# Second part of a perceiver kernel: one block for both parts, matmul work in slots of one gated unit, two chunks routed a slot

## The chip, the cores and the metric

The kernel runs on one core of a Trainium2 chip. A core has five engines that run their own instruction streams and meet at semaphores: PE (TensorE, matmuls), ACT (ScalarE), DVE (VectorE), POOL (GpSimd) and SP (SyncE), which here only issues DMAs. DMAs move data between HBM and the on-chip memory (SBUF); matmuls write to eight banks of PSUM. The metric is device time of one execution in microseconds (us), lower is better.

## The reference

One layer of a perceiver on 64 sequences of 32 tokens with D = 256, all in float32. It has three residual steps; the third, called part 2 here, is what the change is about:

```
x = x + xattn(layernorm(x), ctx)        # cross attention to 257 context rows and the own 32
x = x + mix_and_moe(layernorm(x))       # recurrent time mix, then 8 experts, 2 a token
x = x + ffn(layernorm(x))

geglu(x, w1, w2, w3) = gelu(x @ w1) * (x @ w2) @ w3
def ffn(xf):                            # xf: 2048 tokens x 256
    shared = geglu(xf, w1s, w2s, w3s)   # 256 -> 1024 -> 256
    idx = argmax(xf @ Wg)               # one of 8 experts
    final = sum over e of where(idx == e, geglu(xf, W1[e], W2[e], W3[e]), 0)
    return shared + final
```

## The kernel before

Tokens are worked on in 16 chunks of 128. A first block does the attention, the mix and the 39 tiles of the second step's experts, whose results go to a table rows_y in HBM. It ends with a clearing of its semaphores and a barrier of all engines (L1466). Part 2 follows in three more blocks.

A **unit** is the gated work on 128 tokens: `hidden` on PE (two halves, each of 8 matmuls for x @ w1 and then 8 for x @ w2; the profile counts two records a matmul, so 64 in all), `gelus` on ACT, `products` on DVE (L1708), `down` on PE (L1715, 8 matmuls, 16 records). There are 16 shared units, one a chunk, and 23 routed units, one for each tile of 128 places in the lists of the experts, since lists are rounded up to whole tiles. That makes 39 units.

*Block C* goes over the chunks one at a time, in 18 steps. For chunk a, POOL copies two columns of row numbers (L1754) and gathers the two expert results of the chunk from rows_y (L1757, ya and yb). DVE adds them, weighted, to x (L1810, L1813), takes mean and variance (L1816 to L1821), POOL raises to the power -0.5 (L1762), and DVE writes the normed chunk z (L1828). PE transposes z (L1777), ACT copies it to zT_c (L1800), PE multiplies by the router's matrix (L1785), and DVE copies the 8 scores (L1834). SP stores z to rows_z. On PE the order inside a step is: hidden of the chunk before, transposes of this chunk, down of the chunk before that, router of this chunk. The loop does 12 shared units; four chunks' transposed inputs are kept for later.

*Block `routing`* (L1487 on) takes all scores at once: the largest, the ranks inside each expert, the numbers of tiles, and the table of each tile's tokens, which PE builds with matmuls of one-hot matrices (L1546). One shared unit runs on PE between its steps. No routed unit can start before its end, as neither its expert nor its tokens are known.

*Block F* runs one shared unit, the 23 routed ones, then two shared ones. SP loads the three matrices of a tile's expert, 1 MB each (L1893). POOL gathers a tile's rows from rows_z (zr, ahead by up to four), PE transposes them, and hidden and down follow. Results go to rows_f. POOL gathers from it for all 16 chunks, when the last tile is stored (L1931), DVE adds (L2018), and SP stores the output (L1913).

The loops are written with `sweep`, which peels some steps and runs the rest in a hardware loop; the order on each engine is as written in `body`, and no planner moves it.

## Time and profile before

| | us |
|---|---|
| median of 3 runs (lowest to highest) | 973.64 (972.09 to 974.47) |
| the profiled execution, its own time | 966.43 |
| its span | 964.7 |
| first hidden of part 2 starts | 498.84 |
| last down of part 2 ends | 954.2 |
| PE busy in the span | 858.3 |

The span goes from the first to the last instruction of the profiled execution; 1.7 us of its own time lie around it. The median of the runs shown is 7.2 us above it. The profile has a row of the matmul clock that the chip granted, in tenths or as a fraction of full speed, and a row of how busy the 16 DMA engines were. Rows of the timeline give the start, the busy time, the engine, the source line and the operation; in brackets stands how long the engine had been idle and what ended that. A matmul's modelled end overlaps the start of the next, so lengths are best read from start to start.

### The profile page before, as it was taken

What the parts mean: (1) busy time and instruction counts of PE and PEld (TensorE: products, weight loads), DVE (VectorE), ACT (ScalarE), POOL (GpSimd) and SP (SyncE); (2) the same over time, 40 slices, a digit from 0 to 9 for tenths busy, and PEclk for the clock granted to TensorE, in tenths of its full rate; (3) what the DMA queues carried; (4) which work ended last, traced back from release to release, by engine and by line L of the source; (5) the groups of instructions that cost most, each with busy time, mean ns of one, the idle gap of its engine ahead of it and who ended that gap; (6) DMA issues with size and microseconds to landing.
All of it is one profiled execution on the core that took longest, in us unless ns stands there. A gap on an engine that the chain in (4) does not pass through costs nothing. (4 is left out here: it accounts for less than half of the span.)

```text
span 964.7 us, 19179 instructions
## 1 busy us (share of the span) xinstructions
PE 858.3 (89%) x6306; PEld 768.6 (80%) x6306; DVE 445.0 (46%) x1253; ACT 316.3 (33%) x712; POOL 349.3 (36%) x605
## 2 busy tenths in 40 slices
PE   5899989886667999999949999968999999999994
PEld 4567766665566889999849999957999999999993
DVE  1279989888774555555523333353111111111113
ACT  1466767664542445555411111100111111111110
POOL 1445677766775355544142222211100010000006
PEclk9899999998688989999979999989999999999998
DMA  9875557534612322263121111102998988999716
GB/s 355 277 268 189 194 112 233 155 103 188 169 43 53 79 67 83 83 214 84 50 66 33 34 38 40 38 28 73 336 330 305 329 301 324 303 319 306 270 61 175
DMA packets 92096, 161.79 MB, mean 168 GB/s; under 512 B 13832, under 2 KB 71112, under 8 KB 88680
## 3 DMA queue, kind: packets, MB, share of 16 engines
q1 hardware_dynamic: 71008, 103.39, 32.2%
q10 hardware_dynamic: 12832, 37.82, 10.5%
q0 software_dynamic: 8176, 19.57, 7.9%
q8 instruction: 43, 0.70, 0.3%
q14 instruction: 37, 0.30, 0.1%
HBM read 146.10 MB, written 14.66 MB: 167 GB/s over the span
## 5 line engine op out<-in xcount | busy, mean ns | idle before, releaser
L1691 PEld LDWEIGHTS bank<-zT_f,we 128*128 128x128 f32 x1472 | 167.9, 192 | 1.8 <-ACT zT_f L1979 0.7
L1691 PE MATMUL bank<-zT_f,we 128*128 128x128 f32 x1472 | 168.2, 275 | 0.5 <-ACT zT_f L1979 0.5
L1708 DVE TENSOR_TENSOR hT_f<-bank,act_g 128x512 f32<-128x512 f32 x78 | 53.8, 691 | 227.6 <-PE bank L1691 208.0
L1700 ACT ACTIVATE act_g<-bank 128x512 f32<-128x512 f32 x78 | 46.6, 597 | 320.4 <-PE bank L1691 320.4
L1691 PE MATMUL bank<-zT_c,a_x 128*128 128x128 f32 x1024 | 121.4, 281 | 0.3 <-PEq L1521 0.3
L1691 PEld LDWEIGHTS bank<-zT_c,a_x 128*128 128x128 f32 x1024 | 119.2, 197 | 0.8 <-issue 0.7
L361 POOL DMA_INDIRECT arena_a<-rows_e,pick x78 | 76.0, 975 | 29.8 <-issue 29.8
L410 PE MATMUL bank<-arena_b,arena_a 128*128 128x128 f32 x624 | 81.8, 288 | 1.6 <-DVE hT L546 1.6
L1715 PE MATMUL bank<-we,hT_f 128*128 128x256 f32 x368 | 83.2, 379 | 0.0
L410 PEld LDWEIGHTS bank<-arena_b,arena_a 128*128 128x128 f32 x624 | 78.2, 204 | 2.4 <-DVE arena_b L538 2.4
L1715 PEld LDWEIGHTS bank<-we,hT_f 128*128 128x128 f32 x368 | 68.1, 190 | 8.3
L437 PE MATMUL bank<-arena_a,hT 128*128 x312 | 73.8, 379 | 0.7 <-DVE arena_a L552 0.7
L1920 POOL COPY pick_f<-table 128x1 uint32 (+1 forms) x23 | 4.2, 184 | 186.3 <-PE bank L1941 159.1
L437 PEld LDWEIGHTS bank<-arena_a,hT 128*128 128x128 f32 x312 | 59.2, 190 | 9.2 <-issue 1.1
L1715 PE MATMUL bank<-t_w,hT_f 128*128 128x256 f32 x256 | 59.9, 388 | 3.7 <-DVE hT_f L1708 3.7
L827 PE MATMUL bank<-arena_b,t_w 128*128 128x128 f32 x384 | 55.3, 298 | 6.8 <-DVE arena_b L1230 3.5
L827 PEld LDWEIGHTS bank<-arena_b,t_w 128*128 128x128 f32 x384 | 49.7, 207 | 13.0 <-issue 13.0
L1715 PEld LDWEIGHTS bank<-t_w,hT_f 128*128 128x128 f32 x256 | 48.6, 195 | 10.5 <-DVE hT_f L1708 4.3
L538 DVE SCALAR_TENSOR_TENSOR arena_b<-arena_b,mu_e 128x128 f32<-128x128 f32 x156 | 44.4, 347 | 6.5 <-issue 6.3
L464 ACT ACTIVATE arena_a<-arena_a 128x1024 f32 x39 | 41.2, 1057 | 10.7 <-issue 10.6
L1762 POOL TENSOR_TENSOR rs<-var,eps_pow 128x1 f32<-128x1 f32 x16 | 9.1, 571 | 93.2 <-DVE var L1821 93.2
L1931 POOL DMA_INDIRECT x<-rows_f,slot x16 | 15.5, 970 | 73.5 <-DMA rows_f<-yr 68.9
(273 smaller groups left out, 1361.8 us busy)
## 6 DMA issues: line engine op xcount, KB each, us to landing
we<-in_W_dram SPq DMA_DIRECT2D x69, 1024.0 KB, 7.4
arena_a<-in_ctx_n_dram ACTq DMA_DIRECT2D x16, 1152.0 KB, 7.2
arena_a<-in_ctx_t_dram SPq DMA_DIRECT2D x16, 1028.0 KB, 9.0
rows_y<-arena_a ACTq DMA_DIRECT2D x39, 128.0 KB, 1.7
arena_a<-in_w_moe_dram ACTq DMA_DIRECT2D x3, 1156.0 KB, 5.3
arena_a<-in_w_moe_dram ACTq DMA_DIRECT2D x3, 1152.0 KB, 7.5
rows_f<-yr ACTq DMA_DIRECT2D x23, 128.0 KB, 6.3
rows_e<-arena_b SPq DMA_DIRECT2D x64, 32.0 KB, 4.0
```

Source lines behind the costliest of these rows:

```text
L361: nc.gpsimd.indirect_dma_start(out=pair[:, n % NM, i * D:(i + 1) * D], out_offset=None, in_=rows_e.ap()[0:rows + 1, :], in_offset=bass.Ind ...
L410: last = nc.tensor.matmul(bMH[:, f * P:(f + 1) * P], wk_e[:, n % 2, k * FK + f * P:k * FK + (f + 1) * P], xk[:, n % 2, k * P:(k + 1) * P], ...
L437: last = nc.tensor.matmul(bMY[:, 0:D], hT[:, n % 2, f * P:(f + 1) * P], ewv_sb[:, e, f * D:(f + 1) * D], start=f == 0, stop=f == FKC - 1)
L464: nc.scalar.activation(wk_e[:, n % 2], ewk_sb[:, e], ACT.Copy).then_inc(m_awk, 1)
L538: last = nc.vector.scalar_tensor_tensor(o[:, n % 2, h], diffT[:, n % 2, h], mu_e[:, n % NM, i, k:k + 1], prevT[:, n % 2, h], ALU.mult, ALU ...
L827: last = nc.tensor.matmul(bank[:, m * P:(m + 1) * P], t_w[:, i, k, m * P:(m + 1) * P], xm[:, n % 2, i, k], start=k == 0, stop=k == KD - 1)
L1691: last = nc.tensor.matmul(bank[half][:, f * P:(f + 1) * P], w12[:, i, k, col0:col0 + P], zT[:, k], start=k == 0, stop=k == KD - 1)
L1700: nc.scalar.activation(act_g[:, half], bU[half][:], ACT.Gelu).then_inc(self.ac_g, 1)
L1708: nc.vector.tensor_tensor(hT[:, parity, half * HH:(half + 1) * HH].rearrange("p f t -> p (f t)"), bG[half][:], act_g[:, half], ALU.mult).t ...
L1715: last = nc.tensor.matmul(bY[parity][:, 0:D], hT[:, parity, f], w3[:, f], start=f == 0, stop=f == HC - 1)
L1762: nc.gpsimd.tensor_tensor(rs4[:, b.slot], var4[:, b.slot], eps_pow[:], ALU.pow).then_inc(po_r, 1)
L1931: nc.gpsimd.indirect_dma_start(out=yg[:, c], out_offset=None, in_=rows_f[:, :], in_offset=bass.IndirectOffsetOnAxis(ap=slot2[:, 0, c:c + 1 ...
```

## The change

The three blocks and the barrier go. Part 2 is written as functions that follow the first part's on each engine, inside the same block, with semaphores of its own or counted on. All loops are written out. PE works in 39 **slots** of one unit each: 11 shared, 23 routed, 5 shared. In the first nine slots it also does the routing's work for one **group** of chunks: groups are (0), (1), (2, 3), ... (14, 15), so a slot takes one chunk in slots 0 and 1 and two in slots 2 to 8.

Ranks are now found slot by slot. DVE finds each chunk's expert, and PE multiplies the one-hot mask, and a running sum over earlier chunks, by two constant matrices (`ranks`). That gives a token's rank in its expert's list. POOL scatters the token's number into a table in HBM (tab_f), in which each expert has a region of its own, and SP later reads a tile's 128 numbers from it (pick_rows), which needs where each tile begins (`tile_map`, on DVE in slot 8). In the first part the picks of a tile are counted on other semaphores, and one DMA more zeroes tab_f.

POOL's gathers for group i + 2 run in slot i. The even chunk's two wait for PE's first mark of the slot (g_pe_u, raised when the first quarter of hidden is done), the odd chunk's for the second, three quarters through hidden; the scatters wait for the end of the down of that slot (g_pe_y). The final gathers are marked the same way over the last five slots, and the last chunk's output is added last by `take`.

The diff, cut to its core:

```
-            for i in range(NM):
-                sp.wait_ge(m_put[i], NT1 // NM * 16)
...
-        nc.clear_and_free_semaphores(one_sems)
-        nc.all_engine_barrier()
...
-        SHARED_C = G - KEPT
-            CSTEPS, CPEEL, CTAIL = G + 2, 5, 5
-        routing("r2_", 1, NT2, logits2, False, table2, expert2, slot2, None, None, ge)
...
+        GROUPS = [(0, 1), (1, 2)] + [(c, c + 2) for c in range(2, G, 2)]
+        NGR = len(GROUPS)
+        NT2 = (TOK - E) // P + E
+        SLOTS = ([("s", c) for c in range(NGR + 2)] + [("r", n) for n in range(NT2)]
+                 + [("s", c) for c in range(NGR + 2, G)])
...
+            def pick_rows(n):
+                at = sp.value_load(place2[0:1, n:n + 1], min_val=0, max_val=T_ROWS // P - 1)
+                sp.dma_start(pick2[:, n], tab_f[bass.ds(at * P, P), :]).then_inc(got_pick[n][0], 16)
+            sp.wait_ge(c_dv_map, 1)
+            sp.wait_ge(c_po_tab, 16 * G)
+            for n in range(AHEAD):
+                pick_rows(n)
+            for n in range(NT2):
+                load_w12(n)
+                if n + AHEAD < NT2:
+                    pick_rows(n + AHEAD)
+                if n > 0:
...
+        def part2_pool(pool):
+            for i in range(NM):
+                pool.wait_ge(m_put[i], NT1 // NM * 16)
+            pool.wait_ge(m_row, 1)
+            def gather_sums(g, i=None, half=None):
+                for c in range(*GROUPS[g]):
+                    if half not in (None, c % 2):
+                        continue
+                    if half is not None:
+                        pool.wait_ge(g_pe_u, i * 2 + 1 + half)
+                    for k, t in enumerate((ya, yb)):
+                        nc.gpsimd.indirect_dma_start(out=t[:, c], out_offset=None, in_=rows_y[:, :],
+                                                     in_offset=bass.IndirectOffsetOnAxis(ap=slot1[:, k, c:c + 1], axis=0)
+                                                     ).then_inc(got_sum[g][0], 16)
...
+            def list_rows(g):
...
+                pool.wait_ge(*((g_pe_y, g) if g else (g_pe_g, 2)))
...
+            gather_sums(0)
+            gather_sums(1)
+            rstd(0)
+            for i in range(NGR):
+                if i + 2 < NGR:
+                    gather_sums(i + 2, i, 0)
+                if i + 1 < NGR:
+                    rstd(i + 1)
+                if i + 2 < NGR:
+                    gather_sums(i + 2, i, 1)
+                list_rows(i)
+            pool.wait_ge(c_put, G * 16)
+            for n in range(NT2):
+                pool.wait_ge(*got_pick[n])
...
+            for (lo, hi), (landed, _) in zip(Y_PARTS, got_y):
+                for c in range(lo, hi):
+                    if c % 2 == 0:
+                        half = UNIT_R[NT2 - 1] * 2 + 4 + c // 2
+                        pool.wait_ge(*((g_pe_g, half + 1) if half < 2 * NSLOT - 2 else (g_pe_u, half)))
...
+            def ranks(g):
+                lo, hi = GROUPS[g]
+                pe.wait_ge(c_dv_mask, g + 1)
+                for c in range(lo, hi):
+                    o = bL[:, (2 + c - lo) * E:(3 + c - lo) * E]
+                    nc.tensor.matmul(o, before_m[:], mask2[:, c], start=True, stop=False)
+                    if c > lo:
...
+            transposed(0)
+            pe.wait_ge(ld_s, 16 * 4)
+            router(0)
+            for i in range(NSLOT):
+                hidden(i, 0)
+                if i < NGR:
+                    ranks(i)
+                hidden(i, 1)
+                if i + 1 < NGR:
+                    transposed(i + 1)
+                if in_slot(i + 1, "r") is not None:
+                    transpose_z(in_slot(i + 1, "r"))
+                if i > 0:
+                    down(i - 1)
+                if i + 1 < NGR:
+                    router(i + 1)
+            down(NSLOT - 1)
...
+            combine(0)
+            normed(0)
+            for i in range(NSLOT):
+                if i >= 2:
+                    take(i - 2)
+                if i + 1 < NGR:
+                    combine(i + 1)
+                if i < NGR:
+                    largest(i)
+                products(i, 0)
+                if i == NSLOT - 1:
+                    finish(1)
+                if i < NGR:
+                    places(i)
+                if i + 1 < NGR:
+                    normed(i + 1)
+                if i == NGR - 1:
+                    tile_map()
+                products(i, 1)
+                if i == NGR:
+                    row_numbers()
+                if i == NSLOT - 2:
+                    finish(0)
+            take(NSLOT - 2)
+            finish(2)
+            dve.drain()
+            take(NSLOT - 1)
```

PE before, a shared slot (L1691 hidden, L1777 transposes, L1715 down, L1785 router):

```order
L1691 MATMUL bank<-zT_c,a_x 128x128 x32
L1777 MATMUL bank<-ident,z 128x128 x2
L1715 MATMUL bank<-t_w,hT_f 128x256 x8
L1785 MATMUL bank<-r_w,zT_c 128x8 x2
L1691 MATMUL bank<-zT_c,a_x 128x128 x32
```

PE now, a slot of two chunks (L1641 hidden, one half a row; L1612 to L1615 ranks; L1593 transposes; L1654 down; L1603 router):

```order
L1641 MATMUL bank<-arena_b,a_x 128x128 x16
L1612 MATMUL bank<-mask,before_m 128x8
L1615 MATMUL bank<-earlier,ones_m 128x8
L1612 MATMUL bank<-mask,before_m 128x8
L1614 MATMUL bank<-mask,ones_m 128x8
L1615 MATMUL bank<-earlier,ones_m 128x8
L1641 MATMUL bank<-arena_b,a_x 128x128 x16
L1593 MATMUL bank<-ident,arena_a 128x128 x4
L1654 MATMUL bank<-t_w,arena_b 128x256 x8
L1603 MATMUL bank<-r_w,arena_b 128x8 x4
```

Five small matmuls that need DVE's mask now stand between the halves of hidden, and the transposes and the router's matmuls are doubled.

DVE before, one step of the loop of block C, the same place (L1810 to L1821 the sum and its statistics, L1720 takes a shared unit's result, L1828 z, L1708 the products):

```order
L1810 SCALAR_TENSOR_TENSOR xz<-ya,gate,x 128x256
L1813 SCALAR_TENSOR_TENSOR xz<-yb,gate,xz 128x256
L1816 BN_STATS st<-xz 128x6
L1818 BN_AGGR mv<-st 128x2
L1821 TENSOR_SCALAR var<-mv 128x1
L1720 TENSOR_TENSOR xz<-bank,xz 128x256
L1828 TENSOR_SCALAR z<-xz,mv,rs 128x256
L1708 TENSOR_TENSOR hT_f<-bank,act_g 128x512
```

DVE now, a slot of two chunks up to the first products (L1832 `take`, L1728 to L1739 `combine`, L1751 to L1764 `largest`, L1821 `products`):

```order
L1832 TENSOR_TENSOR xz<-bank,xz 128x256
L1728 SCALAR_TENSOR_TENSOR xz<-arena_a,gate,x 128x256 x2
L1731 SCALAR_TENSOR_TENSOR xz<-arena_a,gate,xz 128x256 x2
L1734 BN_STATS st<-xz 128x6 x2
L1737 BN_AGGR mv<-st 128x2 x2
L1739 TENSOR_SCALAR var<-mv 128x2
L1751 MAX top<-logits 128x8 x2
L1754 MAX_INDEX at<-top,logits 128x8 x2
L1756 TENSOR_TENSOR hot<-iota_e,at 128x16
L1761 CAST mask<-hot 128x16
L1762 TENSOR_TENSOR earlier<-earlier,hot 128x8
L1764 TENSOR_TENSOR earlier<-earlier,hot 128x8
```

The sum and statistics of both chunks of group i + 1 now stand ahead of the search for the largest score of group i, whose mask PE waits for, and both stand ahead of the first products.

## Rows read from the trace of the kernel before

**Rows 1.** The page, part 1: busy us, share, instructions
```profile
PE 858.3 (89%) x6306; PEld 768.6 (80%) x6306; DVE 445.0 (46%) x1253; ACT 316.3 (33%) x712; POOL 349.3 (36%) x605
```

**Rows 2.** The page, part 4: the chain by line
```profile
PE bank L1691 19%; PE bank L1715 9%; DMA x<-rows_f,slot 1%; POOL x L1931 1%; PE bank L1941 0%; DMA rows_f<-yr 0%; DVE xz L2018 0%; DVE hT_f L1708 0%; DVE yr L2006 0%; ACT zT_f L1979 0%; POOLq L1883 0%; DVEq L1705 0%
```

**Rows 3.** Windows: busy of PE, PEld, DVE, ACT, POOL; granted clock, DMA share, GB/s
```profile
core 0: us, PE busy (x) PEld busy (x) DVE busy (x) ACT busy (x) POOL busy (x), PEclk, DMA share, GB/s
509.29:633.38 124.09, 124.09 (x948) 119.45 (x947) 43.57 (x114) 17.36 (x33) 30.48 (x47) 1.00 0.12 36
633.00:668.00 35.00, 22.10 (x137) 19.53 (x135) 19.66 (x99) 2.35 (x5) 3.19 (x4) 0.80 0.07 19
720.76:894.00 173.24, 173.24 (x1315) 166.63 (x1314) 28.91 (x48) 25.24 (x48) 16.10 (x28) 1.00 0.92 315
309.00:342.00 33.00, 28.73 (x169) 25.86 (x168) 20.98 (x62) 13.81 (x24) 12.48 (x18) 0.86 0.28 62
354.50:402.70 48.20, 48.20 (x322) 44.61 (x322) 26.84 (x71) 24.27 (x41) 28.59 (x40) 1.00 0.27 83
```

**Rows 4.** Timeline of PE, one shared slot (start, us, engine, line, operation)
```profile
531.85 7.39 PE L1691 MATMUL bank<-zT_c,a_x 128*128 128x128 f32 x64
539.08 0.38 PE L1777 MATMUL bank<-ident,z 128*128 128x128 f32 x2
539.29 3.62 PE L1715 MATMUL bank<-t_w,hT_f 128*128 128x256 f32 x16
542.75 0.51 PE L1785 MATMUL bank<-r_w,zT_c 128*128 128x8 f32 x4
543.11 7.39 PE L1691 MATMUL bank<-zT_c,a_x 128*128 128x128 f32 x64
```

**Rows 5.** Timeline where the second part starts; idle before and releaser in brackets
```profile
484.72 0.42 DVE L552 TENSOR_TENSOR arena_a<-bank,sig 128x256 f32<-128x256 f32 x1 [2.29 <-PE bank L437]
489.48 0.99 POOL L1757 DMA_INDIRECT ya<-rows_y,pick_c  x1 [0.50 <-POOL pick_c L1754]
493.51 0.48 DVE L1810 SCALAR_TENSOR_TENSOR xz<-ya,gate,x 128x256 f32<-128x256 f32 x1 [8.37 <-DMA yb<-rows_y,pick_c]
496.68 1.32 POOL L1757 DMA_INDIRECT ya<-rows_y,pick_c  x1 [0.28 <-POOL pick_c L1754]
498.84 9.02 PE L1691 MATMUL bank<-zT_c,a_x 128*128 128x128 f32 x64
```

**Rows 6.** The page, part 6: DMA issues, KB each, median us to landing
```profile
rows_y<-arena_a ACTq DMA_DIRECT2D x39, 128.0 KB, 1.7
ya<-rows_y,pick_c POOLq DMA_INDIRECT x16, 2.8
```

**Rows 7.** Timeline of DVE, POOL in a shared slot
```profile
528.76 0.48 DVE L1810 SCALAR_TENSOR_TENSOR xz<-ya,gate,x 128x256 f32<-128x256 f32 x1
530.65 0.15 DVE L1821 TENSOR_SCALAR var<-mv 128x1 f32<-128x1 f32 x1
530.89 0.57 POOL L1762 TENSOR_TENSOR rs<-var,eps_pow 128x1 f32<-128x1 f32 x1 [6.64 <-DVE var L1821]
531.69 0.42 DVE L1720 TENSOR_TENSOR xz<-bank,xz 128x256 f32<-128x256 f32 x1 [0.89 <-PE bank L1715]
```

**Rows 8.** Groups of DVE by form, first part: busy, mean ns, idle before
```profile
L1290 DVE MAX8 top<-logits 128x8 f32<-128x8 f32 x16 | 2.6, 160 | 7.8 <-ACT logits L1119 7.3
L1293 DVE FIND_INDEX8 top_at<-top,logits 128x8 uint32<-128x8 f32 x16 | 2.6, 160 | 0.0
L1296 DVE TENSOR_TENSOR hot<-iota_e,top_at 128x16 f32<-128x16 f32 x16 | 6.0, 376 | 1.2
```

**Rows 9.** Timeline of PE where it leaves the routing pause
```profile
662.29 0.60 PE L1546 MATMUL bank<-r_hot_cp,r_hot_r 128*128 128x46 bf16 x16 [4.35 <-DVE r_hot_cp L1641]
```

**Rows 10.** Timeline of the tail, PE then DVE
```profile
950.48 3.72 PE L1715 MATMUL bank<-t_w,hT_f 128*128 128x256 f32 x16 [3.03 <-DVE hT_f L1708]
962.13 0.43 DVE L2018 TENSOR_TENSOR xz<-xz,x 128x256 f32<-128x256 f32 x1 [0.92 <-DMA x<-rows_f,slot]
```

More of the change, by code:

```diff
@@ L309, in perceiver_block @@
         TA = 9
+        PICKED = ((0, 1), (1, 2), (2, 3), (3, 6), (6, TA), (TA, TA + 1), (TA + 1, TA + 2), (TA + 2, TA + 6), (TA + 6, TA + 15), (TA + 15, NT1))
+        m_pick = [sem1(f"m_pick{i}") for i in range(len(PICKED))]
         assert 2 * CUT - E + 1 >= TA
@@ new lines, in perceiver_block @@
+        NF, NZ = 2, NM
+        rows_z = nc.dram_tensor("rows_z", [TOK, D], F32).ap()
+        rows_f = nc.dram_tensor("rows_f", [NT2 * P, D], F32).ap()
+        in_a = Carve(arena_a, FLOATS_A)
+        we12 = in_a.take(NF, 2 * KD * H).rearrange("p w (i k h) -> p w i k h", i=2, k=KD)
+        we3 = in_a.take(NF, HC, D)
+        ya, yb = (in_a.take(G, D) for _ in range(2))
+        in_b = Carve(arena_b, FLOATS_B)
+        zT_c = in_b.take(G, KD, P)
+        hT_f = in_b.take(2, HC, P)
+        act_g = in_b.take(2, HH * P)
@@ new lines, in perceiver_block, with counted_on @@
+        c_po_r, c_po_tab = sems1("c_po_r c_po_tab")
+        f_sum, f_out = sems1("f_sum f_out")
+        Y_PARTS = ((0, 8), (8, 12), (12, G))
+        AHEAD = 3
+        def counted_on(sems, parts, first, sizes):
+            count = list(first)
+            for i, n in enumerate(sizes):
+                count[i % parts] += 16 * n
+                yield sems[i % parts], count[i % parts]
+        after_moe = [NT1 // NM * 32] * NM
+        got_all = list(counted_on(m_got, NM, after_moe, [2 * (hi - lo) for lo, hi in GROUPS] + [1] * NT2))
@@ L2034, in laid_out @@
+                part2_vector(dve)
 def laid_out(inputs):
```

872 lines of the change are left out of this document (333 added, 539 removed).

## The prediction

> **What bounds the kernel now.** I read four views in this order: busy shares and the chain, windows over stretches of part 2, PE's timeline slot by slot, and the timelines of DVE and POOL at the two ends. PE is busy 858.3 of 964.7 us [rows 1], and the chain that ended last lies on its hidden and down matmuls, 19% and 9%, with about 1% each for the last gather and its issue [rows 2]. Inside stretches PE is full: 124.09 of 124.09 us in the looped shared units, 173.24 of 173.24 in 16 routed ones, at full clock [rows 3]. So what can be won is PE's time in matmuls that aren't units, and its idle time at three places: the hand-over to part 2, the pause for routing, and the tail.
>
> A shared slot costs 7.23 us for hidden, 0.21 for the transposes, 3.46 for down, 0.36 for the router, by starts: 11.26 [rows 4]. A routed one costs 173.24 / 16 = 10.83, or 10.62 without its transposes. The 39 units are thus 414 us of PE whatever the order. PE's part 2 runs from 498.84 [rows 5] to 950.48 + 3.72 = 954.2 [rows 10], 455.4 us; 41 of these are not units. 10.5 more follow to the end of the span.
>
> Of the 41: the pause has 35.00 - 22.10 = 12.9 us idle at a mean clock of 0.80, and one wait of 4.35 for a one-hot product just before its end [rows 3, 9]. Fourteen or so slots pay 0.6 for transposes and router; the first hidden takes 9.02 against 7.39 [rows 5, 4]; the tail has a wait of 3.03 [rows 10].
>
> **The hand-over.** DVE finishes the last tile of part 1 at 484.72 + 0.42 and its store takes 1.7 to land [rows 5, 6], so about 486.9. POOL's first gather starts at 489.48, after barrier, waits and a copy [rows 5]. Now there is neither barrier nor copy, POOL itself waits for the store: 487.3, 2.2 earlier. Behind it nothing changes in kind (gather, sum, power, z, transposes, copy), so the first hidden starts at 498.84 - 2.2 = 496.6. In part 1 the order stays; the added zeroing of the table is one small DMA beside others and I cost it at nothing.
>
> **A slot with two chunks.** Take t = 0 where hidden begins. PE gets to ranks at 3.6, half of 7.23. They need DVE's mask. DVE starts with `take`, released by the down before: 0.42 [rows 7], over by -0.1, as it starts before t = 0. `combine` of two chunks follows. For one chunk it is 530.65 - 528.76 + 0.15 = 2.04 [rows 7]. Two in a row share the waits for results between dependent instructions: ends are 2 x 2.04 = 4.1 less two waits of 0.1, and four sums of 0.40 with two statistics, two aggregates and the add at their bare time, 2.9. I take 3.3, so t = 3.2. `largest` is two maxima and two index searches of 0.16, a one-hot of 0.376 (a row of the same form) [rows 8], and three small ones, a cast and two adds, which no row shows at this size; I give them 0.2 each from the 0.15 of the add [rows 7]. With four waits of 0.09 that is 1.8, t = 5.0, and PE runs at 5.1. So PE stalls 1.5 us in the middle of hidden; bounds from the two ends above are 0.5 and 2.3. That is a new wait, and behind it hidden's second half, down and the next `take` are all late by it, so it can't be caught up: the next slot begins in the same phase.
>
> PE's slot is then 7.23 + 1.5 + 0.15 (five matmuls of 8 columns; a bound from above is the router's 0.36) + 0.44 (four transposes) + 3.46 + 0.72 = 13.5. Slots 2 to 7 have this: 81.0. Slot 1 has one chunk to rank and two to sum, whose gathers were issued last; I give it 14.0 with a stall of 2. Slot 0 has no down and runs at a cold clock, 9.02 for hidden, with small parts 10.6. Slot 8 only ranks: 10.8. Slots 9 and 10 are 10.6 and 10.8.
>
> Is DVE's other work hidden? Per slot it has besides some 1.4 for products, 0.5 for `places`, 0.9 for two z and 0.1 waits: 8.5 us busy of 13.5. POOL has four gathers and two scatters of 0.95 to 1.32 and a power of 0.57 [rows 5, 7]: 8.2 of 13.5. The odd pair of gathers is marked at t = 7.1 (with the stall), its second starts by 8.3 and lands 2.8 after that [rows 6], at 11.1; it is needed when `combine` begins at 13.4. The slack is 2.3.
>
> **Weighed against the skill.** The row at 496.68 shows a gather's issue of 1.32, where others took 0.95 to 0.99, beside DVE's work [rows 5]. The Trainium skill, page "SBUF — State Buffer", section "Who interferes with whom", says that a DVE instruction with two inputs in SBUF and a GpSimd one that reads SBUF exclude each other for their whole length. By it the four sums, 0.48 each, would hold POOL's even pair up by 1.9 us a slot; by the row it is 0.37 at most. Either way the sum stays, and the slack of 2.3 shrinks to 0.4 by the page; that is why I do not put the second rival lower.
>
> **From slot 9 on.** The scatter's last landing, SP's read of the first three lists, the gather of the first tile and its matrices all have to come before slot 11's hidden. Last scatters are issued 1.8 into slot 9; with three landings of about 3 us each in a row (nearest row 2.8 [rows 6]) the first tile is there at some 15 of the 21.4 us of slots 9 and 10. Its 2 MB come about 11 us after `tile_map`, at 19.5. So the pause is gone, with 2 us to spare. `tile_map`, about 3.5 us of small DVE instructions (an estimate by count at 0.2 each), stands in slot 8 between z and the second products; it delays down by at most 0.8, and down comes a slot later.
>
> Routed: 22 x 10.83 + 10.62 = 248.9. The list of a tile now comes by a DMA of 128 rows of 4 bytes. In part 1 such picks are in 309 to 342: DMA share 0.28 at 62 GB/s, against 0.27 at 83 GB/s where there are few [rows 3]. By bytes 0.20 was due, so 0.08 x 33 us = 2.6 for 30 picks, 0.09 each. DMA now has 0.92 x 10.83 = 9.96 a slot; 10.05 is still under 10.83, so the cost is nothing. Five shared units at 10.6: 53.0; the last down 3.5; small restarts of PE, 0.1 in seven slots: 0.7.
>
> A page has another price for the pick: the Trainium skill, "DMA: Bandwidth & Descriptors", section "Bandwidth", gives 0.68 us for 4 KB over 128 partitions issued by GpSimd. An estimate from it is 9.96 + 0.68 = 10.64, hidden still, but with 0.2 to spare; this bears on the third rival.
>
> **The tail.** All gathers but the last chunk's come before PE's end, marked over five slots. Behind the last down stand `take` 0.42, 0.15 between, and the output's DMA, 964.7 - 962.13 - 0.43 = 2.1 [rows 10]: 2.7 in place of 10.5. The wait of 3.03 goes too, since `finish` stands behind the products.
>
> **Sum.** 496.6 + 10.6 + 14.0 + 81.0 + 10.8 + 10.6 + 10.8 + 248.9 + 53.0 + 3.5 + 0.7 = 940.5 for PE's end, against 954.2: 2.2 from the start and 11.5 from slots (30 not units in place of 41; 11 of these are the new stalls). With 2.7 the span is 943.2, 21.5 less. The profiled execution was 1.7 over its span and the median 7.2 over that: 944.9 and 952.
>
> **Rivals.**
> First, no stall: `combine` and `largest` are over by 3.6. Two chunks would need 1.4 less of DVE than worked out; nothing speaks for it but that the waits between instructions are a guess. Eleven us less: 942.
> Second, the gathers come later than `combine`: POOL blocked by DVE, or the landing slower under more traffic. DVE's idle of 8.37 for the first gather [rows 5] shows that such a wait lands whole. At 4 us late, 1.7 beyond the slack, in seven slots it is 12 us: 964. Late lists or matrices at slot 11 cost about as much.
> Third, on the other side: routed slots become bound by DMA. It is at 0.92 [rows 3], so a slot may take 0.87 more before PE waits. The picks, SP's issues, and instruction fetch of a program without loops would have to add more than that; to be slower than now, a routed slot must go from 10.83 to 11.8 or more (21.5 / 22 = 0.98), 1.8 more of DMA work. At 12.2 it is 30 us: 982. Against it: 0.09 a pick.
> Fourth, the change doesn't bring what it says: the pause only moves to slot 11, as the first tile's chain is longer than two slots, and the stalls are at 2.3: some 973.
>
> **Chances.** The forecast 0.68, first rival 0.10, second 0.14, third 0.05, fourth 0.03. By the stall's bounds (seven slots by -1.0 to +0.8) and the hand-over's, the forecast's own range is 943 to 962; to 940 and 966 it takes in the first rival and the second. The measurement tells 0.3%, 2.9 us. Below 970.7: forecast and first two with one in a hundred off, 0.91. Above 976.6: 0.05. Between: 0.04.
>
> **What would show it.** PE's first hidden at about 496.6; a wait of some 1.5 for DVE's mask between two halves in slots 2 to 7, slots 13.5 apart; no gap before slot 11, routed slots at 10.8 with clock 1.00; 2.7 us from PE's end to the span's. It is wrong if the routed slots are longer than 11, if DVE waits for gathers in slots 2 to 7, or if a gap of over 3 us stands at slot 11.

## The result and the profile after

| kernel | runs | median us | lowest to highest |
|---|---|---|---|
| before | 4 | 974.0 | 972.09 to 974.47 |
| after | 4 | 956.79 | 955.88 to 957.87 |

The ratio is 0.9827 (95% interval 0.981 to 0.9845), 17.2 us less. The forecast was 952, its range 940 to 966. The profiled execution has a span of 954.6 and took 956.36.

PE's busy time, from part 1 of the page of the kernel after, is that of before [rows 1] to 0.3 us, so no work of PE went away and the gain is time in which PE stood idle:

```profile
PE 858.6 (90%) x6328; PEld 769.0 (81%) x6328; DVE 443.8 (46%) x1278; ACT 316.8 (33%) x714; POOL 355.4 (37%) x572
```

A window over slots 2 to 7, which take two chunks each (it begins 4.4 us early, in slot 1), and one over 16 routed units (columns as in rows 3):

```profile
core 0: us, PE busy (x) PEld busy (x) DVE busy (x) ACT busy (x) POOL busy (x), PEclk, DMA share, GB/s
523.50:611.00 87.50, 79.51 (x606) 75.49 (x604) 42.28 (x164) 12.47 (x25) 35.72 (x38) 0.98 0.44 52
711.68:884.78 173.10, 173.10 (x1314) 166.49 (x1312) 28.93 (x48) 25.29 (x48) 12.42 (x13) 1.00 0.91 311
```

The routed units take 10.82 us each at full clock with the DMA engines 0.91 busy, where the kernel before had 0.92 [rows 3]. The slots with two chunks move 52 GB/s at a DMA share of 0.44, where the looped shared units moved 36 at 0.12 [rows 3]. That is over twice as much engine time for a byte, and it was not forecast.

PE's timeline of the kernel after, slots 0 to 7 (L1641 hidden, L1612 the first matmul of the ranks, in brackets its wait for the mask):

```profile
502.39 6.34 PE L1641 MATMUL bank<-arena_b,a_x 128*128 128x128 f32 x32
...
519.47 0.18 PE L1612 MATMUL bank<-mask,before_m 128*128 128x8 bf16 x1 [2.05 <-DVE earlier L1764]
...
527.89 3.82 PE L1641 MATMUL bank<-arena_b,a_x 128*128 128x128 f32 x32
532.34 0.18 PE L1612 MATMUL bank<-mask,before_m 128*128 128x8 bf16 x1 [0.64 <-DVE earlier L1764]
...
553.84 3.82 PE L1641 MATMUL bank<-arena_b,a_x 128*128 128x128 f32 x32
560.80 0.18 PE L1612 MATMUL bank<-mask,before_m 128*128 128x8 bf16 x1 [3.14 <-DVE earlier L1764]
...
560.94 5.45 PE L1641 MATMUL bank<-arena_b,a_x 128*128 128x128 f32 x32
...
575.81 0.18 PE L1612 MATMUL bank<-mask,before_m 128*128 128x8 bf16 x1 [1.07 <-DVE earlier L1764]
...
589.20 0.18 PE L1612 MATMUL bank<-mask,before_m 128*128 128x8 bf16 x1 [1.07 <-DVE earlier L1764]
...
602.90 0.18 PE L1612 MATMUL bank<-mask,before_m 128*128 128x8 bf16 x1 [1.38 <-DVE earlier L1764]
```

Slot 2 waits 0.64 for the mask, the shortest wait of the seven. Slot 4 waits 3.14, and its second half takes 5.45 against 3.82: after the wait the granted clock is 0.68 (560.9 to 566.3), where it is 1.00 in slots 2, 3 and 5. With 2.05 in slot 1 and 0.69 in slot 3 the waits come to 10.0; the prediction had 11.0. The hand-over, and the end:

```profile
489.94 0.42 DVE L511 TENSOR_TENSOR arena_a<-bank,sig 128x256 f32<-128x256 f32 x1 [2.29 <-PE bank L395]
...
492.93 0.96 POOL L1533 DMA_INDIRECT arena_a<-rows_y,slot  x1 [23.45 <-DMA rows_y<-arena_a]
...
497.09 0.48 DVE L1728 SCALAR_TENSOR_TENSOR xz<-arena_a,gate,x 128x256 f32<-128x256 f32 x1 [6.73 <-DMA arena_a<-rows_y,slot]
...
500.29 0.69 PE L1593 MATMUL bank<-ident,arena_a 128*128 128x128 f32 x2 [10.39 <-DVE arena_a L1744]
```

```profile
952.03 0.42 DVE L1832 TENSOR_TENSOR xz<-bank,xz 128x256 f32<-128x256 f32 x1 [1.50 <-PE bank L1654]
```

From the last result of part 1 (L511, at 490.36 over) to the first hidden (502.39) are 12.0 us, in place of 13.7 [rows 5]. PE ends at 952.0, the span 2.6 later.

From the end of part 1 to the end of the span the changed kernel's profile is 15.3 us shorter. These are 1.7 at the hand-over, 5.8 between PE's first hidden and its last down (449.6 in place of 455.4), and 7.9 behind it (2.6 in place of 10.5), so the largest piece is the tail.

Part 1 ended 5.2 us later than in the profile of before, 490.4 against 485.1. To see whether this belongs to the change, and to have a measure that is free of it, the table gives for each run the end of part 1 and the **length of part 2**: from there to the end of the span. Both are of one execution, the profiled one; a ratio compares medians with those of the kernel before that was timed beside the same run.

| kernel | median us | ratio to before (95%) | end of part 1 | part 2 |
|---|---|---|---|---|
| before | 974.0 | | 485.1 | 479.6 |
| before, again | 962.62 (one) | | 481.5 | 479.4 |
| after | 956.79 | 0.9827 (0.981 to 0.9845) | 490.4 | 464.2 |
| after, again | 947.04 | 0.9801 (0.9762 to 0.984) | 482.7 | 460.7 |
| largest first | 945.18 | 0.9761 (0.9734 to 0.9789) | 484.9 | 461.2 |
| few scatters | 947.26 | 0.9786 (0.9757 to 0.9815) | 487.1 | 460.6 |
| scatters last | 963.77 | 0.9927 (0.99 to 0.9954) | 489.4 | 472.2 |
| scatters last, largest first | 958.20 | 0.9871 (0.9837 to 0.9906) | 487.7 | 469.9 |
| twelve and four | 950.48 | 0.9792 (0.9762 to 0.9821) | 488.0 | 459.0 |
| fourteen and two | 962.06 | 0.9923 (0.9895 to 0.9952) | 487.5 | 472.8 |
| gathers three ahead | 947.06 | 0.9799 (0.9773 to 0.9825) | 487.3 | 461.4 |
| all three edits | 936.33 | 0.9697 (0.9671 to 0.9723) | 485.0 | 448.2 |
| more picks | 956.51 | 0.9906 (0.9873 to 0.9938) | 486.4 | 469.0 |
| more gathers | 962.73 (one) | | 484.7 | 476.3 |

### The profile page after: what moved, and what is told of

It is laid out like the page before. It is cut to its first block, busy times and chain, and to the rows that moved or that the text cites. A ratio compares the mean times of both kernels' runs of the same rounds, so it can differ in the third digit from the quotient of the medians.

```text
span 954.6 us, 18843 instructions
## 1 busy us (share of the span) xinstructions
PE 858.6 (90%) x6328; PEld 769.0 (81%) x6328; DVE 443.8 (46%) x1278; ACT 316.8 (33%) x714; POOL 355.4 (37%) x572
## 3 DMA queue, kind: packets, MB, share of 16 engines
q10 hardware_dynamic: 12832, 37.82, 10.5%
## 4 chain that ended last, share of the span: by engine, by line
PE 60%; DVE 13%; issue 6%; DMA 6%; DVEq 6%; POOL 6%; ACT 1%; another core or an unknown queue 1%; ACTq 1%; SPq 0%; POOLq 0%
PE bank L1641 24%; PE bank L1654 13%; PE bank L368 7%; PE bank L395 6%; PE bank L382 3%; DMA arena_a<-rows_y,slot 2%; DMA xz<-in_x_dram 2%; DVEq L1386 2%; DVE arena_b L1189 1%; PE bank L357 1%; PE bank L777 1%; POOL arena_a L1533 1%; POOL tab_e L683 1%; DMA tab_f<-token,listed 1%
## 5 line engine op out<-in xcount | busy, mean ns | idle before, releaser
L1641 PEld LDWEIGHTS bank<-arena_b,arena_a 128*128 128x128 f32 x1472 | 167.9, 192 | 2.6 <-issue 1.5
L1641 PE MATMUL bank<-arena_b,arena_a 128*128 128x128 f32 x1472 | 168.1, 275 | 1.1 <-issue 1.1
L1821 DVE TENSOR_TENSOR arena_b<-bank,arena_b 128x512 f32<-128x512 f32 x78 | 54.0, 692 | 208.7 <-PE bank L1641 198.4
L1705 ACT ACTIVATE arena_b<-bank 128x512 f32<-128x512 f32 x78 | 46.6, 598 | 305.9 <-PE bank L1641 300.8
L1641 PE MATMUL bank<-arena_b,a_x 128*128 128x128 f32 x1024 | 123.9, 282 | 0.0
L1641 PEld LDWEIGHTS bank<-arena_b,a_x 128*128 128x128 f32 x1024 | 121.0, 198 | 0.4
L368 PE MATMUL bank<-arena_b,arena_a 128*128 128x128 f32 x624 | 82.3, 289 | 1.6 <-DVE hT L505 1.6
L1654 PE MATMUL bank<-arena_a,arena_b 128*128 128x256 f32 x368 | 83.2, 379 | 0.0
L368 PEld LDWEIGHTS bank<-arena_b,arena_a 128*128 128x128 f32 x624 | 78.6, 205 | 2.5 <-DVE arena_b L497 2.4
L1654 PEld LDWEIGHTS bank<-arena_a,arena_b 128*128 128x128 f32 x368 | 68.1, 190 | 8.3
L786 PEld LDWEIGHTS bank<-arena_b,t_w 128*128 128x128 f32 x384 | 48.2, 202 | 13.5 <-issue 13.5
L1654 PE MATMUL bank<-t_w,arena_b 128*128 128x256 f32 x256 | 57.7, 379 | 0.0
L1654 PEld LDWEIGHTS bank<-t_w,arena_b 128*128 128x128 f32 x256 | 47.5, 190 | 5.8
L1533 POOL DMA_INDIRECT arena_a<-rows_y,slot x32 | 31.3, 978 | 55.1 <-PE bank L1641 24.1
```

Source lines behind the costliest of these rows:

```text
L368: last = nc.tensor.matmul(bMH[:, f * P:(f + 1) * P], wk_e[:, n % 2, k * FK + f * P:k * FK + (f + 1) * P], xk[:, n % 2, k * P:(k + 1) * P], ...
L786: last = nc.tensor.matmul(bank[:, m * P:(m + 1) * P], t_w[:, i, k, m * P:(m + 1) * P], xm[:, n % 2, i, k], start=k == 0, stop=k == KD - 1)
L1533: nc.gpsimd.indirect_dma_start(out=t[:, c], out_offset=None, in_=rows_y[:, :], in_offset=bass.IndirectOffsetOnAxis(ap=slot1[:, k, c:c + 1] ...
L1641: last = nc.tensor.matmul(bank[half][:, f * P:(f + 1) * P], w12[:, i, k, col0:col0 + P], zT[:, k], start=k == 0, stop=k == KD - 1)
L1654: last = nc.tensor.matmul(bY[u % 2][:, 0:D], hT_f[:, u % 2, f], w3[:, f], start=f == 0, stop=f == HC - 1)
L1705: nc.scalar.activation(act_g[:, half], bU[half][:], ACT.Gelu).then_inc(g_ac_g, 1)
```

## The experiments

**The two kernels again.** No edit.

> The kernel before, unchanged. The profiled execution of before had a span of 964.7 us while its median of 974.0 lies 9.3 us above that; the kernel after had 954.6 and 956.8, only 2.2 apart, and its last tile of the first part ended 5.2 us later (490.4 against 485.1). Theory A: the first part of both kernels is the same and varies by several us between executions; this profile then has a span of some 970 to 972 and the last tile of part 1 ends at 490 to 492. Theory B: the added zeroing DMA and the other waits made part 1 slower by 5 us; then this profile repeats 485 and 965.

> The changed kernel, unchanged, as the base of the runs beside it. Theory A (execution variance in part 1): its part 1 ends at 487 to 492. In slots 2 to 7 PE's wait for the mask is 0.6 to 0.7 where DVE does not wait for gathers, and larger where it does. Whether slot 4's wait of 3.14 us comes again at the same place tells a cause in the data or code from chance. Time 955 to 958.

Part 1 ended at 481.5 and 482.7, earlier than either theory's figures, so neither came as written. That it varies between executions is shown: the changed kernel's own two profiles are 7.7 apart there. Whether the change also slows it is less clear. Part 1 ends at 486.8 on average in the twelve profiles below that have the change, and at 483.3 in the two of before. Against a slowing, the medians in the two sets that have both kernels differ by 17.2 and 20.6 (967.6 and 947.04, ratio 0.9801, 0.9762 to 0.984), no less than part 2 by itself (15.3 and 18.7). A difference of a few us can't be excluded. Part 2 is 479.6 and 479.4 before and 464.2 and 460.7 after. The waits for the mask were 2.04, 0.63, 0.67, 2.22, 1.07, 0.67, 2.05: slot 4's is large again, the ones of slots 6 and 7 changed.

**Largest scores first** (DVE's order):

```diff
+                if i < NGR:
+                    largest(i)
                 if i + 1 < NGR:
                     combine(i + 1)
-                if i < NGR:
-                    largest(i)
```

> DVE finds the largest scores of group i before it sums group i + 1, so the mask is ready at 2.0 us into the slot where PE wants it at 3.6. Theory A (PE stalls because DVE does the sums first, and waits for their gathers there too): the waits for the mask, 10.0 us in seven slots, go; what is late next is z of the next group for the transposes, at about 7.6 against 7.4, so 0.2 to 0.5 a slot, and more where gathers land late. Sum 6 to 9 us faster than the changed kernel, 948 to 951. Theory B (DVE is the bound of these slots): the stall moves from the mask to the transposes in full, and the time is within 2 us of the changed kernel.

No wait for the mask was left, and yet part 2 took 461.2, and the median is 1.9 less than that of the kernel after beside it. Rows of its timeline (POOL L1533 gather, L1550 scatter; DVE L1728 the sum; PE L1593 transposes of z):

```profile
552.91 0.96 POOL L1533 DMA_INDIRECT arena_a<-rows_y,slot  x1 [0.30 <-issue]
...
557.14 1.00 POOL L1550 DMA_INDIRECT tab_f<-token,listed  x1 [3.27 <-PE bank L1654]
...
567.31 0.88 DVE L1728 SCALAR_TENSOR_TENSOR xz<-arena_a,gate,x 128x256 f32<-128x256 f32 x2 [7.91 <-DMA arena_a<-rows_y,slot]
...
572.47 1.11 PE L1593 MATMUL bank<-ident,arena_a 128*128 128x128 f32 x4 [7.36 <-DVE arena_a L1744]
```

The gather issued at 552.91, in slot 4, is what DVE waits for until 567.31, in slot 5: of the 64 marks that the group's four gathers raise, 63 stand at 562.50 and the last at 567.28. The PE wait behind it, 7.36, took what the order had won. Theory B's time came (within 2 us), but not its reason: the stall did not move to the transposes slot by slot, the time went in one late landing. Slot 4 waits 0.54 here, for z.

**Few scatters.** Groups 1 to 7 scatter nothing, so the tiles gather other rows, and SP waits for the three scatters that are left; nothing else is left out.

```diff
                 pool.wait_ge(c_dv_slot, g + 1)
+                if 1 <= g <= 7:
+                    return
```

> Leaves out the scatters of token numbers of groups 1 to 7 (POOL's list_rows), so tiles gather the wrong rows; the amount of other work is the same. In the changed kernel DMA engines were 0.4 to 0.65 busy in slots 2 to 7 at only 50 to 60 GB/s, where the kernel before had 0.12 at 36, and in slots 4 and 5 the gathers' landing was what DVE waited for. Theory A (the scatters of 4-byte elements ahead of the gathers in POOL's queue hold their transfers up): the DMA share of slots 2 to 7 falls to 0.2 or less, the odd pair lands some 3 us after its issue, DVE no longer waits for gathers, and PE's waits for the mask come to 0.6 each: 3 to 5 us faster, 952 to 954. Theory B (the gathers are slow by themselves, by their number or by DVE's work beside POOL): shares and waits stay, within 1 us.

The window of slots 2 to 7, and PE's waits for the mask (us in total, times, longest):

```profile
520.00:598.00 78.00, 73.84 (x584) 70.23 (x583) 41.32 (x162) 11.84 (x24) 24.58 (x27) 1.00 0.19 59
```

```profile
PE bank L1614 <- DVE earlier L1766: 6.2, 7, 2.0
```

The DMA share is 0.19 at 59 GB/s, against 0.44 at 54 in the same stretch of the changed kernel beside it, and slots 2 to 6 wait 0.64 or 0.65 each, slot 7 0.94. So with the scatters of 128 numbers of 4 bytes the slow transfers and the late gathers go. POOL's smaller load is not the reason: in slot 3 it issues the last gather 3.6 us after the second half of hidden starts with the scatters (541.25 and 537.62, the run of the kernel after beside it), and 4.3 after without them (546.54 and 542.29). Part 2 is no shorter than in the run beside it (460.6, 460.7), though: 3.1 us less of waits for the mask, but PE waited 3.06 for the first tile's rows (most tokens are row 0 there) and ran the next down in 4.95, at a granted clock of 0.72. The time of this kernel therefore says nothing; its slots do.

**Scatters last.** All scatters but group 8's go behind the last gathers.

```diff
-                list_rows(i)
+                for g in {NGR - 3: range(5), NGR - 2: range(5, NGR - 1), NGR - 1: [NGR - 1]}.get(i, ()):
+                    list_rows(g)
```

> The scatters of token numbers of groups 0 to 7 (16 with group 8's) leave the slots in which results are gathered and go behind the last gathers, to slots 6 to 8, where POOL has room. All work stays. Theory A (a gather issued behind a scatter lands late): DMA share in slots 2 to 6 falls from 0.44 to about 0.19 as in the run without scatters, PE waits 0.64 for the mask in each of slots 2 to 7 and 2.0 in slot 1, where the changed kernel had 9.4 to 10 in all: 6 us in all, so 3 to 4 us faster than the changed kernel. The table is complete at the same place in slot 9, so slot 11 is as before. Theory B (the run without scatters was quicker in these slots only because POOL had less to do): the waits stay above 1 us in slots 4 to 7.

Its slots did what theory A says: 0.60 to 0.67 in slots 2 to 6, 6.2 in all. That is theory A for these slots. But part 2 is 472.2, 8.0 to 11.5 longer than in the kernel after, because of something neither theory had. PE's timeline in slots 6 and 7, ACT's gelus and DVE's products in the latter, a window of 10 us there, and PE's waits:

```profile
583.16 0.18 PE L1613 MATMUL bank<-mask,before_m 128*128 128x8 bf16 x1 [0.61 <-DVE earlier L1765]
...
598.42 0.48 PE L1642 MATMUL bank<-arena_b,a_x 128*128 128x128 f32 x2 [0.43 <-issue]
600.83 0.81 PE L1642 MATMUL bank<-arena_b,a_x 128*128 128x128 f32 x3 [1.93 <-issue]
...
600.87 0.60 ACT L1706 ACTIVATE arena_b<-bank 128x512 f32<-128x512 f32 x1 [8.85 <-remote]
...
604.98 0.37 PE L1642 MATMUL bank<-arena_b,a_x 128*128 128x128 f32 x1 [3.34 <-issue]
...
610.14 0.69 DVE L1822 TENSOR_TENSOR arena_b<-bank,arena_b 128x512 f32<-128x512 f32 x1 [13.75 <-remote]
```

```profile
600.00:610.00 10.00, 2.53 (x8) 2.10 (x9) 0.00 (x0) 0.60 (x1) 3.06 (x4) 0.50 0.02 1
```

```profile
PE bank L1642 <- issue: 10.6, 9, 3.3
...
PE bank L1613 <- DVE earlier L1765: 6.2, 7, 2.1
```

POOL issued twelve scatters back to back from 588.2 to 604. PE stood still in pieces, in the middle of a run of matmuls whose inputs all were there: nine waits between 597.2 and 616.2, 10.8 us in all, for nothing that the profile shows, with the DMA engines 0.02 busy, and at a granted clock of 0.50 in the window. (The view's 10.6 and a further 1.4 at L1655 make 12.0; 1.15 of these stand at the first routed unit, as in the kernel after.)

PE's marks came late too. The matmul that lets ACT begin the first gelu of slot 7 starts at 593.41; ACT begins at 600.87. "Remote" is a releaser outside the profile, but the trace has the times at which semaphores rise: this mark stands at 600.85, and the next, of the matmul at 595.20, at 610.06. In slot 3 of the kernel after the mark of the matmul at 549.03 stands at 549.32.

> Both edits: scatters behind the last gathers, and the largest scores found ahead of the sums. With largest first alone two places waited, one of them 7.4 us for a gather that took 14 us to land behind a scatter. Theory A: that wait goes with the scatters, and the waits for the mask with the order: no wait over 0.3 us in slots 2 to 8, slots of 11.9; 9 to 10 us faster than the changed kernel in part 2. Theory B (the late gather had another cause, such as writes of rows_z): a wait of several us for gathers comes again in some slot, and the gain is under 6.

The same edit with the largest scores first: no wait for the mask or a gather at all, and 12.3 us of the other kind in nine pieces (1.8 more at the first routed unit). So late gathers do go with the scatters, and the pauses come with them in a row. The median is 5.6 below that of the run before it, and still above that of the kernel after in ratio, so the forecast gain of 9 to 10 did not come.

**A burst of gathers** in place of one of scatters: twelve gathers to a buffer no longer read, eight after the scatters of group 6 and four ahead of those of group 7. It was executed once.

```diff
+            def more(chunks):
+                for c in chunks:
+                    nc.gpsimd.indirect_dma_start(out=yb[:, c], in_=rows_y[:, :], ...).then_inc(more_got, 16)
...
+                if i == NGR - 2:
+                    more(range(8, 12))
                 list_rows(i)
+                if i == NGR - 3:
+                    more(range(8))
```

> The changed kernel with twelve more gathers of 128 KB by POOL back to back, in slots 6 and 7, to a buffer no longer read; scatters stay where they were. In the run with the scatters moved, twelve scatters in a row stood in these slots and PE waited 12 us in ten pieces for nothing that the profile shows, in the middle of hidden and down. Theory A (pending 4-byte writes hold up the fetch of PE's instructions): twelve gathers in their place cause no such waits, under 2 us in all. Theory B (any burst of POOL's transfers starves the fetch): 8 us or more of such waits in slot 7.

PE's waits of 490 to 700 begin with these, and none is of the kind with no releaser:

```profile
PE bank L1604 <- DVE arena_a L1755: 15.2, 2, 10.4
PE bank L1623 <- DVE earlier L1775: 13.0, 7, 5.8
```

The longest wait for the mask, 5.8, is in slot 4, ahead of the burst. The 15.2 is the first z (10.4) and one of 4.86 for the z of group 8, whose power stood behind eight gathers in POOL's queue. So this burst of POOL's transfers doesn't stop PE in pieces, and the burst of 4-byte writes does. The two differ in direction (reads against writes of HBM) and in size, 1 KB against 4 bytes a row; which of the two matters was not tried.

The expectation's theory A says that the writes hold up the loading of PE's instructions. The traces don't bear this out. In the run with the scatters last, the queues that load instructions brought nothing of 16 KB between 594.99 and 624.78, and two packets of 8 KB, over at 597.43 and 605.59; yet PE's pauses end at nine different times from 597.7 to 616.1. What fits better is that signals are late: two of PE's marks stood 7 and 15 us late, and marks of the twelve scatters still came at 616 to 619, although POOL had issued the last at 603.00. Why PE itself pauses stays open.

**Twelve and four; fourteen and two** shared units ahead of and behind the routed ones:

```diff
-        SLOTS = ([("s", c) for c in range(NGR + 2)] + [("r", n) for n in range(NT2)]
-                 + [("s", c) for c in range(NGR + 2, G)])
+        SLOTS = ([("s", c) for c in range(NGR + 3)] + [("r", n) for n in range(NT2)]
+                 + [("s", c) for c in range(NGR + 3, G)])
...
-                        half = UNIT_R[NT2 - 1] * 2 + 4 + c // 2
+                        half = 2 * NSLOT - 8 + c // 2
```

(NGR + 5 in the second, and the final sums behind the last products.)

> Twelve shared units ahead of the routed ones and four behind, in place of eleven and five. In the changed kernel PE waited at slots 10 and 11 for the first tile's rows (1.5) and 1.1 more before its first routed unit. Theory A (the chain table, list, rows and matrices is longer than two slots by 1 to 3 us): with one slot more it is hidden, no gap before the first routed unit, 1.7 to 2.6 us faster, and the tail stays at 2.6 as four units still cover sixteen gathers of 1.3. Theory B (the gap is POOL's or SP's own cost, or the tail needs all five units): no gain, or a wait for the last gathers of more than 1 us.

> Fourteen shared units ahead and two behind the routed ones, as in the kernel before; the final sums stand behind the last products on DVE. It undoes the part of the change that puts five last. After the store of the last tile (some 3 us into slot 38) POOL still has sixteen gathers of 1.27, 20 us, and PE only 11. Theory A (five last hid the tail): the span's end comes 10 to 11 us after PE's, in place of 2.6, and the gap at the first routed unit goes (2.6), so 5 to 8 us slower than the changed kernel. Theory B (the tail was short for another reason, the single last sum): under 2 us slower.

What they are about is PE's wait at the first routed unit in the kernel after, and the chain to it (start, us, what):

```profile
641.73 0.41 PE L1624 MATMUL bank<-ident,arena_b 128*128 128x128 f32 x2 [1.51 <-DMA arena_b<-rows_z,pick]
641.97 3.62 PE L1654 MATMUL bank<-t_w,arena_b 128*128 128x256 f32 x16
646.70 7.38 PE L1641 MATMUL bank<-arena_b,arena_a 128*128 128x128 f32 x64 [1.11 <-issue]
653.92 0.38 PE L1624 MATMUL bank<-ident,arena_b 128*128 128x128 f32 x2
```

```profile
624.03 7.54 DMA tab_f<-token,listed
...
632.36 2.59 DMA pick<-tab_f
...
635.72 5.87 DMA arena_b<-rows_z,pick
...
641.73 0.41 PE bank L1624 x2
```

The last scatter takes 7.54 to land, the list 2.59, the rows 5.87. With twelve ahead PE has no wait there, and the tail stays (937.36 + 7.07 to 947.0: 2.6). Part 2 is 459.0, 1.7 to 5.2 less, with 8.6 for the mask in place of 9.4 and 10.0: theory A in the profile. In the medians it doesn't show: the ratio, 0.9792 (0.9762 to 0.9821), can't be told from 0.9801 and 0.9827. With two behind, DVE's last sums stand here, PE having ended at 943.4:

```profile
945.37 2.77 DVE L1838 TENSOR_TENSOR xz<-xz,x 128x256 f32<-128x256 f32 x8 [4.90 <-DMA x<-rows_f,slot]
...
957.75 0.42 DVE L1832 TENSOR_TENSOR xz<-bank,xz 128x256 f32<-128x256 f32 x1
```

The tail is 16.9, more than the 10 to 11 that were expected; part 2 is 13.8 longer than with four, and the median 11.6. That is what four units last are worth against two, with DVE's final sums moved behind the last products as well, which this run does not separate.

**Gathers three groups ahead:**

```diff
+            gather_sums(2)
             for i in range(NGR):
-                if i + 2 < NGR:
-                    gather_sums(i + 2, i, 0)
+                if i + 3 < NGR:
+                    gather_sums(i + 3, i, 0)
```

(and the odd chunk's alike)

> The changed kernel with its gathers of expert results one group further ahead: group i + 3 in slot i, at the same marks, and group 2 ahead of slot 0; scatters stay in pairs where they were. Theory (the waits for the mask above 0.65 in slots 4 to 7 are gathers that land late behind or beside scatters; in the run with largest first one took 14 us): with a slot more to land DVE never waits for them; slots 2 to 7 stall 0.64 each, slot 1 under 1 as its group is there too: 4.5 to 5 in all against 9.4 to 10, 4 to 5 us faster. Rival (late landing is not it, DVE's or PE's own instruction supply is): waits of 1 to 3 us stay in some slot.

DVE never waited for a gather in the slots, as forecast, and slots 2, 3, 5, 6 wait 0.59 to 0.67, slot 1 0.26, slot 7 0.94. But slot 4 waits 3.02 again, and part 2 is 461.4, as in the kernel after, so the 4 to 5 us did not come and the rival did. Slot 4 here (PE, DVE, PE):

```profile
549.09 4.26 PE L1642 MATMUL bank<-arena_b,a_x 128*128 128x128 f32 x32
...
551.27 0.42 DVE L1833 TENSOR_TENSOR xz<-bank,xz 128x256 f32<-128x256 f32 x1 [5.57 <-remote]
...
556.37 0.19 PE L1613 MATMUL bank<-mask,before_m 128*128 128x8 bf16 x1 [3.02 <-DVE earlier L1765]
```

DVE's take, ACT's copy and POOL's scatter all begin at 551.3 to 551.5, 2 to 3 us later in the slot than elsewhere, though PE's down had ended at 548.4; the mark of its last matmul stands at 551.25, 2.8 late. So here slot 4 is a late mark of PE, as in the run with the scatters last, and no late gather.

In the other kernels with scatters in these slots and the old DVE order it is a gather. Slot 4 waits 1.8 to 5.8 for the mask in them, and 0.6 in the two without scatters there. In five of the six DVE's wait in front of the sums is put down to the gathers, 1.1 to 5.1 us; this is the run of the kernel after, again:

```profile
547.34 0.88 DVE L1728 SCALAR_TENSOR_TENSOR xz<-arena_a,gate,x 128x256 f32<-128x256 f32 x2 [1.55 <-DMA arena_a<-rows_y,slot]
```

In the first profile of the kernel after, whose wait of 2.44 has no releaser, the last mark of these gathers stands at 554.81, so about half of it is a late gather too. Loads of instructions are slow in the same place: the packet of 16 KB there takes 4.65 us, and 0.96 in the run with few scatters. Such packets take 3.8 and 4.0 in the run with all three edits, in which nothing stalls, so they are not shown to cost anything. Why slot 4 is the worst stays open.

**All three** (largest first, gathers three ahead, twelve and four):

> Three edits at once: gathers three groups ahead, largest scores ahead of the sums, and twelve shared units before and four behind the routed ones. No wait for the mask (10 us in the changed kernel), none for gathers, none for the first tile (2.6). What is late next is z of the next group, at most 0.3 a slot. From the end of part 1 to the span's end 460.7 to 464.2 us in the changed kernel: here 449 to 453, so some 11 us faster. Rival: the burst of PE's waits that came with scatters in a row comes with shorter slots too; then 456 or more.

It takes 936.33, ratio 0.9697 (0.9671 to 0.9723) to before, and part 2 448.2, a little better than expected. DVE's `take` in slots 4 to 6 shows the slots' length, 12.1 to 12.2:

```profile
543.85 0.42 DVE L1833 TENSOR_TENSOR xz<-bank,xz 128x256 f32<-128x256 f32 x1 [2.78 <-PE bank L1655]
...
556.02 0.42 DVE L1833 TENSOR_TENSOR xz<-bank,xz 128x256 f32<-128x256 f32 x1 [3.16 <-PE bank L1655]
...
568.16 0.42 DVE L1833 TENSOR_TENSOR xz<-bank,xz 128x256 f32<-128x256 f32 x1 [3.13 <-PE bank L1655]
```

Their parts are 7.3 + 0.15 + 0.44 + 3.46 + 0.81: no stall is left in them. It is 12.5 to 16.0 shorter in part 2 than the kernel after, and the fastest of all.

**More picks** (three more reads of each list):

```diff
                 sp.dma_start(pick2[:, n], tab_f[bass.ds(at * P, P), :]).then_inc(got_pick[n][0], 16)
+                for j in range(3):
+                    sp.dma_start(spare[:, n * 3 + j], tab_f[bass.ds(at * P, P), :]).then_inc(more_got, 16)
```

> Each tile's list is read four times in place of once, three of them to a spare buffer: 69 DMAs more of 128 rows of 4 bytes, three a routed slot of 10.82, of which the DMA engines were busy 0.91. Theory A (a pick costs 0.09 us of the engines, as estimated from part 1): 10.1 of 10.82, routed slots stay at 10.82 and the time of the changed kernel within 1 us. Theory B (the Trainium skill, page DMA: Bandwidth & Descriptors, 0.68 us for 4 KB): 9.85 + 2.0 = 11.9 a slot, some 20 us slower. Theory C: SP's issue of three more DMAs, about 1.1 us each, delays the next load of matrices past its time: a wait for weights of under 2 us a slot.

```profile
720.00:890.00 170.00, 170.00 (x1286) 163.39 (x1286) 28.74 (x48) 24.67 (x47) 12.38 (x13) 1.00 0.90 310
```

Share 0.90 where it was 0.91, PE full: three more picks a slot cost the engines nothing that can be seen. By my 0.09 a pick the share would be 0.02 to 0.03 higher, and by the 0.68 that the Trainium skill gives (page "DMA: Bandwidth & Descriptors", section "Bandwidth") it would pass 1, so neither applies beside loads of matrices. What it did cost is at one place, the first routed unit, where nine more picks stand ahead of the first loads on SP and three more ahead of the second:

```profile
645.04 9.82 PE L1645 MATMUL bank<-arena_b,arena_a 128*128 128x128 f32 x64 [5.88 <-issue]
```

With the hidden behind it at a granted clock of 0.74 (9.82 in place of 7.38) this is theory C at one place, and more than its 2 us: part 2 is 469.0, 4.7 and 8.3 longer than in the two profiles of the kernel after.

## Why the prediction was right, step by step

- **The total is nearer than its parts, and part of that is luck.** PE's end was forecast at 940.5 and came at 952.0: 5.2 of part 1, 0.6 at the hand-over and 5.7 in the slots. Against it, I added 8.9 from span to median and 2.2 was due, since the profiled execution of before was a short one (its median lies 7.2 above it, that of after only 0.4). So 11.5 too little and 6.7 too much leave nearly the 4.8 between 952 and 956.79.
- **Hand-over**: 2.2 forecast, 1.7 measured. The first hidden was to start at 496.6 and started at 502.39, as part 1 ended 5.2 later; that lies within what part 1 varies between executions.
- **The stall**: 1.5 a slot forecast, 0.64 measured where nothing else is late. Part of the difference is how it is counted: by starts the undisturbed slots take 12.95 and 13.00, 0.8 over the slot without stall (12.16), where I had 13.5. The sums took 3.2 us where I had 3.3 (540.57 to 543.79), but began 0.27 ahead of hidden, and the search took 1.6, not 1.8. The total, 10.0 against 11.0, came out right by luck: a second cause that I had only as a rival, gathers that land late, made up for the shorter stall, most of it in slot 4. The order of DVE alone was not what bounded these slots; taken away by itself (largest first) it gave 1.9 us of median, and together with the twelfth unit 10.7 (all three edits against the lead alone, which was timed beside it).
- **Lower clock**: 1.6 us in slot 4 (5.45 in place of 3.82), not in the sum.
- **From slot 9 on**: this term failed. I gave the scatter, the list and the rows about 3 us each; they took 7.54, 2.59, 5.87, and PE waited 1.51 and 1.11. I took one price for three transfers from a gather's row [rows 6], and neither the scatter nor the rows came at it. The two slots were 2 us to spare in the forecast and 2.6 short in the trace.
- **Routed units** 248.9 forecast, 248.7 measured; the five shared and the last down 56.5 and 56.6; tail 2.7 and 2.6.
- **My own signs**: "it is wrong if DVE waits for gathers in slots 2 to 7" came true, in slots 5 to 7 of the kernel after and, in its second profile, in slots 4, 5 and 7. The routed slots (10.82) and the gap before the first routed unit (2.6, under 3) did not. So the time came as forecast, and this part of the mechanism did not.
- **The range**: its upper end, 962, is not reached by its own terms (952 + 5.6 for the stall + 2.2 for the hand-over is 959.8).
- **Rivals**: the second (gathers later than the sums) came in part, 3 to 4 us of waits in slots 4 to 7, with scatters as the cause and not POOL blocked by DVE. The page "SBUF — State Buffer" of the Trainium skill, section "Who interferes with whom", as I read it, would have held POOL up for the sums' length; the trace has two scatters beside them at 1.00 and 1.09 (0.99 to 1.01 for the others in these slots), here the second:

```profile
540.57 0.87 DVE L1728 SCALAR_TENSOR_TENSOR xz<-arena_a,gate,x 128x256 f32<-128x256 f32 x2
...
541.78 1.09 POOL L1550 DMA_INDIRECT tab_f<-token,listed  x1 [0.30 <-issue]
...
553.23 0.42 DVE L1832 TENSOR_TENSOR xz<-bank,xz 128x256 f32<-128x256 f32 x1 [2.78 <-PE bank L1654]
...
556.10 0.91 DVE L1728 SCALAR_TENSOR_TENSOR xz<-arena_a,gate,x 128x256 f32<-128x256 f32 x2 [2.44 <-issue]
```

The last of these rows is the wait of 2.44 in slot 4. The third rival didn't come (share 0.91, 10.82 a slot), nor the first. Of the fourth a little did, the 2.6 before the first routed unit.

All slots together were 449.6 against 443.9 forecast: 0.6 and 0.3 more in slots 0 and 1, 2.5 in slots 2 to 7, 0.1 in slot 8, 3.0 in slot 10, less 0.7 for restarts.

## What to carry to other kernels

When instructions are interleaved by hand, the engine that prepares the next step's work should first finish what another engine waits for now; but see what is late next, since here the order alone gave little until the transfers had a slot more of lead. A scatter of single 4-byte elements is to be priced by the time until it lands and by what it does to transfers beside it, not by its bytes, and many of them in a row are to be avoided: here they stopped PE, which had nothing to do with them. Before a cause is named for such pauses, look whether signals came late. Compare stages from a landmark inside the execution when an earlier, unchanged stage varies more than the change.

## What was not expected of the hardware

- A scatter of 128 numbers of 4 bytes took 7.54 us to land in the kernel after and 6.84 with the scatters last, and with two of them a slot the DMA engines were 0.44 busy for 54 GB/s, in place of 0.19 for 59. A gather beside them took over 14 us once.
- Twelve such scatters in a row stopped PE for 10.8 us in nine pieces while the DMA engines were 0.02 busy; twelve gathers of 128 KB did not. Two of PE's marks rose 7 and 15 us late in that stretch.
- Reads of 128 numbers of 4 bytes cost the DMA engines nothing that shows beside loads of matrices, four a slot (share 0.90).
